# Cross attention: when TensorE sums the accumulated exponentials of a pair of heads

## The reference, cut to what matters

```python
q = (lat @ Wq)   -> 8 batches, 16 heads, 512 rows, 64
k, v = split(ctx @ Wkv)  -> 8 batches, 16 heads, 1024 rows, 64; k is rotated
attn = einsum('bhnd,bhsd->bhns', q, k) * scale
attn = clip(attn, -11.0, 11.0)
attn = softmax(attn, axis=-1)
out = einsum('bhns,bhsd->bhnd', attn, v)
return out @ Wo + bo
```

## Time and profile before

| | |
|---|---|
| median of three runs | 3120.7 us (3119.66 to 3125.37) |
| the profiled execution | 3130.13 us, span 3128.4 us |
| TensorE busy | 2871.6 us, 92% of the span |
| VectorE busy | 2198.0 us, 70% |
| GpSimd busy | 1581.4 us, 51% |
| ScalarE busy | 1435.1 us, 46% |
| granted TensorE clock, mean | 0.973 |

### The profile page before, as it was taken

One profiled execution on the slowest core, in us unless ns is written; L12 is line 12 of the kernel. 1 busy time (PEld: TensorE's weight loads), 2 busy tenths in 40 slices (PEclk: granted clock), 3 DMA queues, 4 the chain that ended last, 5 costly groups with the idle time before them and its releaser, 6 DMA issues. The chain is left out here.

```text
span 3128.4 us, 52086 instructions
## 1 busy us (share of the span) xinstructions
PE 2871.6 (92%) x17208; PEld 1966.8 (63%) x17256; DVE 2198.0 (70%) x3444; ACT 1435.1 (46%) x2076; POOL 1581.4 (51%) x1051
## 2 busy tenths in 40 slices
PE   5999999969999999999999999999999969999994
PEld 4888888854554554554454455455455359899984
DVE  3555555558788778778778777777877864588875
ACT  2222222245554554554554654554544532465554
POOL 1222222227447546546546645655645616377765
PEclk9999999989999999999999999999999989999997
DMA  9000000020010010010010010010010033387876
GB/s 263 15 15 15 16 15 15 15 61 14 11 42 11 11 42 11 14 42 8 14 42 8 14 42 8 14 45 7 12 45 8 11 111 130 117 222 218 228 202 179
DMA packets 144519, 180.85 MB, mean 58 GB/s; under 512 B 16992, under 2 KB 106848, under 8 KB 144224
## 3 DMA queue, kind: packets, MB, share of 16 engines
q1 hardware_dynamic: 117808, 145.84, 15.2%
q0 software_dynamic: 14304, 18.75, 3.6%
q10 hardware_dynamic: 12112, 12.48, 1.5%
HBM read 114.35 MB, written 45.90 MB: 51 GB/s over the span
## 5 line engine op out<-in xcount | busy, mean ns | idle before, releaser
L825 POOL TENSOR_SCALAR raw<-raw 128x1024 f32<-128x1024 f32 x416 | 684.2, 1645 | 192.5 <-ACT raw L1080 171.8
L1080 ACT ACTIVATE raw<-b_ps 128x1024 f32<-128x1024 f32 x416 | 410.7, 1021 | 366.6 <-PE b_ps L854 318.6
L967 PE MATMUL b_ps<-raw 128*64 128x512 f32 x1664 | 423.7, 612 | 57.2 <-POOL raw L825 57.2
L1231 DVE TENSOR_TENSOR b_acc<-b_acc,raw 128x1024 f32<-128x1024 f32 x304 | 399.3, 1313 | 89.9 <-POOL raw L825 80.3
L811 POOL TENSOR_TENSOR b_knat<-raw,b_knat 128x512 fp32r<-128x512 f32 x128 | 165.4, 1292 | 404.2 <-ACT b_knat L1034 404.2
L846 PE MATMUL b_ps<-b_QH,b_KT 128*128 128x512 f32 x1024 | 325.2, 430 | 14.8 <-ACT raw L1080 9.1
L846 PEld LDWEIGHTS b_ps<-b_QH,b_KT 128*128 128x128 f32 x1024 | 168.8, 189 | 245.1 <-issue 157.4
L1672 PE MATMUL c_ps<-c_xT_l,c_w_h 128*128 128x256 f32 x1504 | 307.7, 288 | 6.7 <-DVEq L1914 3.2
L967 PEld LDWEIGHTS b_ps<-raw 128*64 128x64 f32 x1664 | 95.4, 135 | 277.3 <-POOL raw L825 160.3
L1204 DVE RECIPROCAL b_r<-b_ps 128x128 f32<-128x128 f32 x256 | 239.2, 945 | 19.9 <-PE b_ps L874 18.4
L1672 PEld LDWEIGHTS c_ps<-c_xT_l,c_w_h 128*128 128x128 f32 x1504 | 245.1, 193 | 12.2 <-issue 6.2
(11 more groups left out here) (260 smaller groups left out, 7080.4 us busy)
## 6 DMA issues: line engine op xcount, KB each, us to landing
c_raw<-in_L_ffn_W_dram SPq DMA_DIRECT2D x117, 512.0 KB, 5.8
b_QH<-b_QH SPq DMA_DIRECT2D x128, 128.0 KB, 2.4
xs<-zeros ACTq DMA_DIRECT2D x1, 10140.0 KB, 65.8
c_xg<-xs SPq DMA_DIRECT2D x39, 260.0 KB, 7.2
b_rows<-in_ctx_dram SPq DMA_DIRECT2D x9, 1024.0 KB, 7.9
a_xt<-in_x_dram SPq DMA_DIRECT2D x72, 64.0 KB, 2.2
b_rows<-x SPq DMA_DIRECT2D x9, 512.0 KB, 7.2
x<-a_x1t SPq DMA_DIRECT2D x64, 64.0 KB, 1.9
```

The source lines that it names most:

```text
L825: pool.tensor_scalar(pr, pr, HI, LO, ALU.min, ALU.max).then_inc(clipped, 1)
L967: mm = pe.matmul(bank(key)[hh * HD:(hh + 1) * HD, :], V[:, t, (2 * p + hh) * HD:(2 * p + hh + 1) * HD], place(unit(p, j, a))[:, hh * B:(hh ...
L1080: ins = act.activation(place(unit(p, j, a)), both(key), ACT.Exp, scale=SCALE)
L1231: dve.tensor_tensor(total, total, pr, ALU.add).then_inc(acc_ready, 1)
```

## The change

The sums of pair p - 1 are made in step 1 of pair p in place of step 0, behind the scores that step makes and ahead of its products with V. The list of bank uses follows. Only pairs 1 to 3 of a group are touched; the sums of the last pair stay where they were.

```diff
                     if (p, j) == (0, 0):
                         order += [(("kt", g, CT - 1, a), 6 + a) for a in range(2)]
+                    if j == 1 and p:
+                        order.append((("sum", g, p - 1), 6))
                     if j == 0:
-                        if p:
-                            order.append((("sum", g, p - 1), 6))
                         if p + 1 < PG:
                             order.append((("q", g, p + 1), 7 if p else 5))
                         order.append((("o", g, p), 4 + p % 2))
...
                                 if (p, j) == (0, 0):
                                     k_turn(g, CT - 1)
-                                if j == 0 and p:
+                                if j == 1 and p:
                                     sums(pe, b, g, p - 1)
                                 if j == 0 and p + 1 < PG:
                                     queries(pe, b, g, p + 1)
```

## The result

The kernel after has a median of 3179.3 us in six runs (3172.4 to 3184.3); that of before, in six runs, 3120.2 (3108.0 to 3125.4). The ratio is 1.0196 [1.0177, 1.0215]: 2.0% slower, 59 us. The prediction had the direction, and was 32 us short in size.

The account below looks back on a forecast made before the run. TensorE was taken to set the pace, with VectorE having little to spare. Eight batches of 1.1 us (group 0) plus 2.2 us (group 1) made 26 us on the 3120.7 us median: 3147 us, 0.8% slower, range 3117 to 3168.

Parts of the forecast that it names:

- The 0.28: Group 0, first pair: TensorE's 0.28 us wait ahead of the moved sums should go, 2.2 us over eight batches.
- Line 1211 appears as a releaser: Sign: `o_scaled` ends TensorE's idle time at pair 3 step 0, about 1.6 us in each group, 25 us in all.
- about 105 us: Sign: VectorE's wait for the sums rises from 18.4 us by 88 us, to some 105.
- 2.5 and 1.8: Group 0, pairs 2 and 3: us by which the sums come late for VectorE's reciprocal.
- The net: Group 0: lateness VectorE carries to the group's end less the 0.28 us won; 0.6 to 1.5, taken as 1.1 us.
- Faster: Rival: clips beside a waiting VectorE run faster, TensorE's waits for them go; 9 us won, 3112 us; chance 0.09.
- 8 x (1.1 + 2.2) = 26 us: Whole kernel: eight batches, each 1.1 us later in group 0 and 2.2 us in group 1.
- 1.5 + 0.7 = 2.2 us: Group 1: 1.5 us of lateness left on VectorE plus 0.7 of a meeting between an addition and a clip.
- the range's upper end: Likeliest case's upper end: meetings of additions with clips make 2.0 us in group 0, 3.6 in group 1; 45 us, 3166.
- Carried and more: Rival: TensorE's 16 new stops also lower its clock, 26 us on top of the carried lateness; about 3173 us; chance 0.07.
- Nothing happens: Rival: VectorE makes up its lateness before pair 1's `o_scaled`; TensorE wins only 2.2 us; 3118.5 us; chance 0.14.
- its decisive point, 0.6 us: Pair 3's first product with V: up to 0.6 us of `o_scaled` lateness holds TensorE no longer than before.

Follow-up runs that it names:

- e1: Changed kernel with the first piece of VectorE's reciprocal of the moved sums one place later, behind the next addition; ratio to the kernel before 0.9997.
- e5: Changed kernel with eight useless matmuls filling TensorE's stop ahead of pair 3's first product with V, in both groups; ratio to the kernel before 1.0142.
- e10: Changed kernel with only pair 3's sums moved and `context_lo` ahead of the waiting reciprocal; ratio to the kernel before 1.0057.
- e2: Changed kernel with the sums moved in pair 3 only, those of pairs 1 and 2 left in step 0; ratio to the kernel before 1.0085.
- e7: Changed kernel with `context_lo` put ahead of the waiting reciprocal in VectorE's queue; ratio to the kernel before 1.0115.
- e6: Changed kernel with the reciprocal's first piece one place later and pair 3's output in bank 7 in place of bank 5; ratio to the kernel before 1.0075.

## Why the prediction was right in direction and wrong in size

**The mechanism: right.** The reciprocal's wait, carried down VectorE's queue, is the cause: without it the whole loss is gone (e1). The 0.28 is gone. Line 1211 appears as a releaser in all 16 groups. VectorE's waits for clips in `raw` ahead of line 1231 fell from 80.3 to 36.7 us. VectorE's wait for sums was to rise to about 105 us, and is 103.0, but that is luck: in group 0 the waits of pairs 2 and 3 are 1.14 and 1.18 us above, where 2.5 and 1.8 were added up, and in e5, where the clock holds at the stop, all of them make 83.4. The slower clock filled the rest: where it falls beside group 0's stop, pair 3's wait is 2.6 to 2.8 us.

**Group 0: the sum right by luck, its parts not.** The net was put at 1.1 us and measured 1.14. Counted from the group's first product with V, `o_scaled` ends 0.44 us later (51.56 against 51.12), where 1.3 was predicted, and yet the stop is 2.30 instead of 1.6. TensorE came there sooner: its scores end 49.38 us into the group, where with the same work done they ended at 50.85 (1220.84 in the earlier trace rows), 1.47 sooner. From pair 1's first product with V up to the stop (1206.23 to 1239.24 us) it is not idle at all, where the earlier trace rows had 0.86 (busy time of that window, columns as there):

```profile
1206.23:1239.24 33.01, 33.01 (x143) 13.09 (x142) 28.36 (x31) 16.65 (x21) 25.44 (x16) 1.00 0.07 16
```

With the 0.28 that is most of the 1.47. So the rival *Faster* was right that the clip waits go, and right in what spoke against it: all of that is handed back at pair 3. The first product there comes at 51.68 us, before at 51.75; with the sum behind it the next step's comes 0.89 late (1246.11 less the 1189.86, against 1225.35 less the 1169.99), where 1.6 was predicted.

**The step that failed is the sum, "8 x (1.1 + 2.2) = 26 us", in two places, the second the larger.**

First, group 1's term. "1.5 + 0.7 = 2.2 us" measured 3.0, which makes some 6 us of the 32. Only two ways from VectorE to TensorE were followed, `o_scaled` and the last addition. The third, over `context_lo` and ScalarE, was missed; what is behind the waiting reciprocal in the queue had not been listed to the end. e10 beside e2 gives its worth, about 1.15 us a batch. And TensorE is 1.28 us late at pair 3 (2542.36 - 2484.98 = 57.38 into the last batch's group against 2486.55 - 2430.45 = 56.10), where 0.7 was predicted. The meetings of additions with clips were undercounted too. The largest form of line 1231 had, in the groups of instructions of before, this row (the mean of one is 1313 ns):

```profile
L1231 DVE TENSOR_TENSOR b_acc<-b_acc,raw 128x1024 f32<-128x1024 f32 x304 | 399.3, 1313 | 89.9 <-POOL raw L825 80.3 <-DVE b_QL L1183 2.4
```

and after it has this one:

```profile
L1231 DVE TENSOR_TENSOR b_acc<-b_acc,raw 128x1024 f32<-128x1024 f32 x304 | 423.5, 1393 | 50.6 <-POOL raw L825 36.7 <-DVE b_QL L1183 7.2
```

24 us more VectorE work, in place of waits for clips that it no longer has. The shared port is here as the Trainium skill, page "SBUF — State Buffer", section "SBUF: two separate sides", states it: the later of the two stands still, and the trace agrees (2.05 us for the addition ahead of `o_scaled`). That was named as the way to the range's upper end.

Second, the clock, for which the sum has no term. *Carried and more* was given 0.07 as a case apart, with 26 us on top, on the ground that a window with 1.12 us of idle time kept its clock. The stops became 2.3 us, twice as long as that, and the last sums' 2.63; about 23 us of clock came on top, of which filling the stop in e5 gave back 17. The price was about right and its chance was not: the clock loss is no alternative to carried lateness but comes with it. With the measured terms, the sum is 8 x (1.1 + 3.0) + 23 = 56 us.

***Nothing happens*** did not, but its decisive point, 0.6 us, was the wrong one. In group 0 `o_scaled` ended only 0.44 us later, inside it, and pair 3's first product was not later (51.68 against 51.75). The loss came all the same, since the sum, 0.9 us of TensorE, was still to be made behind that product. In group 1 the point was passed: TensorE's product is 1.28 us late.

**What stays open.** Why the clock falls at some stops and not at others was not settled. In after half clock begins beside 10 of 16 stops at pair 3, in e1 beside 4 of its 8 of 2.10 us; near the end of group 0 it begins in all 8 batches of after, whose last sums wait 2.63 us, in 6 of 8 in before and in none in e1. So e1 has half the stops, and no half clock behind its last sums of group 0, but what decides at a single stop is open. How the loss divides between the ways to TensorE was measured for the one over ScalarE only. Nor was it tried to fill the wait of 2.63 ahead of the last sums.

## What to carry to other kernels

Moving work to a later place on one engine moves the wait to whoever reads it, and in an in-order queue that wait delays everything behind it: list all of it, with each engine that waits for any of it, and not only the two that one is looking at. What stands behind the wait and needs nothing of it can go ahead of it: that alone gave back 25 of the 59 us (e7). Before a producer is made later, see whether its consumer can be put one place later as well; here one place was enough to make the change free. And where a change gives TensorE new stops, as here of 2.3 and 2.6 us, a loss of clock belongs in the likeliest case, not in one apart.

## What was not expected of the hardware

Useless matmuls in a stop gave back 17 us of the 59 (e5). And where a wait stands can matter more than its length: in e6 a stop of 2.1 us was removed, one of 2.63 appeared at the group's end, the two groups took about the same time, and the kernel lost 24 us, some 19 of them by the granted clock.
